# The adapter rows of half 0 wait for half 0's first values instead of its last scores

## The reference

```
x  = x + attention(conditioned(x, itok))          # 16 heads of 16, causal, softmax
g  = y @ Wg + (y @ Ag[itok]) @ Bg[itok]           # y is the new x, rank 16, 1024 hidden
u  = y @ Wu + (y @ Au[itok]) @ Bu[itok]
h  = silu(g) * u
d  = h @ Wd + (h @ Ad[itok]) @ Bd[itok]
x  = x + fwht(silu(d @ W1.T) * (d @ W3.T)) @ W2.T
```

## Time and profile before

| | |
|---|---|
| runs shown | 215.78, 216.59, 217.85 us; median 216.59 |
| profiled execution, its own time | 217.52 us |
| its span | 215.7 us |
| mean granted TensorE clock | 0.992 |
| busy: TensorE matmuls | 209.0 us (97%) |
| busy: VectorE, ScalarE, GpSimd | 96.2, 93.5, 104.5 us |
| moved by DMA | 16.65 MB, 77 GB/s mean |

### The profile page before, as it was taken

How to read it: one execution, slowest core, us unless ns; L and a number is a source line. 1 busy time by engine, 2 the same in 40 slices (tenths; PEclk the granted TensorE clock), 3 DMA queues, 4 the chain that set the end, 5 groups by cost and what they waited for, 6 DMA issues and landing times.

```text
span 215.7 us, 5107 instructions
## 1 busy us (share of the span) xinstructions
PE 209.0 (97%) x1977; PEld 167.3 (78%) x1977; DVE 96.2 (45%) x173; ACT 93.5 (43%) x162; POOL 104.5 (48%) x120
## 2 busy tenths in 40 slices
PE   7899999799999999999999999999999999999994
PEld 2567787487878788787887888788888888888894
DVE  3798998489545975210211210065942222220211
ACT  2456899446866340623532432322755554430000
POOL 4005788039693613538454349102499999441000
PEclk9999999699999999999999999999999999999999
DMA  5950099646903195031210170300111000000211
GB/s 144 393 205 3 25 145 151 81 150 143 153 0 100 50 155 143 0 104 29 74 28 18 30 310 3 97 0 0 52 41 57 2 0 3 0 0 3 97 49 49
DMA packets 16263, 16.65 MB, mean 77 GB/s; under 512 B 1776, under 2 KB 13040, under 8 KB 15984
## 3 DMA queue, kind: packets, MB, share of 16 engines
q1 hardware_dynamic: 15808, 15.26, 29.5%
q10 hardware_dynamic: 432, 1.07, 1.7%
HBM read 15.27 MB, written 1.05 MB: 76 GB/s over the span
## 4 chain that ended last, share of the span: by engine, by line
PE 92%; DMA 3%; DVE 2%; issue 1%; SPq 0%; ACT 0%
PE bank L479 25%; PE bank L481 23%; PE bank L483 23%; PE bank L636 8%; DMA raw<-w_stream 3%; PE bank L553 2%; PE bank L676 2%; PE bank L579 2%; PE bank L608 1%; PE bank L498 1%; PE bank L533 1%; PE bank L532 1%; PE bank L534 1%; PE bank L543 1%; DVE w_lo L1062 1%
## 5 line engine op out<-in xcount | busy, mean ns | idle before, releaser
L1375 POOL TENSOR_TENSOR h_lo<-tmp_b,h_hi 128x512 fp32r<-128x512 f32 x32 | 42.5, 1348 | 41.8 <-ACT h_hi L887 41.8
L479 PE MATMUL bank<-act_hi,w_hi 128*128 128x512 f32 x144 | 52.6, 402 | 0.1
L481 PE MATMUL bank<-act_lo,w_hi 128*128 128x512 f32 x144 | 51.0, 390 | 0.0
L483 PE MATMUL bank<-act_hi,w_lo 128*128 128x512 f32 x144 | 50.9, 390 | 0.0
L1199 DVE TENSOR_TENSOR tmp_b<-bank,tmp_a 128x512 f32<-128x512 f32 x32 | 20.8, 686 | 61.8 <-ACT tmp_a L894 35.8
L1328 POOL TENSOR_TENSOR w_lo<-raw,w_hi 128x512 fp32r<-128x512 f32 x21 | 26.8, 1290 | 19.7 <-ACT w_hi L822 19.7
L479 PEld LDWEIGHTS bank<-act_hi,w_hi 128*128 128x128 f32 x144 | 27.0, 188 | 7.8 <-issue 0.8
L894 ACT ACTIVATE tmp_a<-bank 128x512 f32<-128x512 f32 x32 | 17.3, 592 | 34.8 <-PE bank L636 30.6
L483 PEld LDWEIGHTS bank<-act_hi,w_lo 128*128 128x128 f32 x144 | 27.0, 188 | 5.8
L481 PEld LDWEIGHTS bank<-act_lo,w_hi 128*128 128x128 f32 x144 | 27.1, 188 | 5.1
L887 ACT ACTIVATE h_hi<-tmp_b 128x512 fp32r<-128x512 f32 x32 | 19.7, 632 | 19.9 <-DVE tmp_b L1199 19.9
(11 more groups left out here) (96 smaller groups left out, 249.8 us busy)
## 6 DMA issues: line engine op xcount, KB each, us to landing
raw<-w_stream SPq DMA_DIRECT2D x24, 256.0 KB, 3.8
b_own<-w_stream SPq DMA_DIRECT2D x32, 128.0 KB, 4.4
k_x<-x_slots ACTq DMA_DIRECT2D x2, 512.0 KB, 6.2
resid<-x_feat SPq DMA_DIRECT2D x1, 1024.0 KB, 8.1
tmp_a<-w_t SPq DMA_DIRECT2D x1, 1024.0 KB, 5.0
out_feat<-tmp_b SPq DMA_DIRECT2D x3, 256.0 KB, 2.1
a_down_raw<-w_stream SPq DMA_DIRECT2D x1, 512.0 KB, 4.3
b_down<-w_stream SPq DMA_DIRECT2D x32, 16.0 KB, 1.6
```

The costliest lines, as they stand in the source:

```text
L479: pe.matmul(ps[:, :], w[0], x_hi, start=start, stop=False)
L481: pe.matmul(ps[:, :], w[0], x_lo, start=False, stop=False)
L483: last.append(pe.matmul(ps[:, :], w[1], x_hi, start=False, stop=stop))
L1375: pool.tensor_tensor(lo, tmp_b[:, n % 4, :], f32(hi), ALU.subtract).then_inc(prod_split, 1)
```

## The change

One wait of the SP queue is another one. The 16 transfers of half 0's adapter rows were issued when the last scores of half 0 were complete; now they are issued when both tiles of half 0's first values (`values(0, 0)`) are complete. In TensorE's list this is six steps later. All else stays, and so does the order in which the SP queue issues.

```
             sp.wait_ge(xc_hi_made, DC + 1)
-            wait_full(sp, "s", 0, TILES_S - 1)
+            wait_full(sp, "y", 0, SLOTS // 2 - 1)
             load_b_own(0, 0, first_half, 0, BH)
             wait_full(sp, "s", 1, TILES_S - 1)
             for m in range(1, 4):
                 load_weights(W_GU + m)
```

## The result

The changed kernel takes 222.22 us (median of four runs, 221.24 to 222.65) against 216.67 us for the kernel before (four runs, 215.78 to 217.85). The ratio is 1.0246, with a 95% interval of 1.0186 to 1.0307: it is slower, by 5.55 us in the medians (whether by more than 2% the interval leaves open), where 3.4 us were forecast and 221.6 was the end of the range. The profiled executions took 222.40 and 217.52 us, with spans of 220.6 and 215.7: 4.9 us apart. Only these 4.9 us can be followed in the rows; the other 0.65 lie in the scatter of the four runs on either side, whose sources the rows cannot show.

A forecast was written before the change was run, and what follows sets the result against it. TensorE was taken to bound the kernel, its matmuls busy 209.0 of 215.7 us. The later gate_up(1, 0), +1.8, and the clock, +1.6, made +3.4 us on the median 216.59: 220.0 us, range 218.2 to 221.6.

The forecast's parts named there:

- What bounds the kernel, and where the gap came from: TensorE bounds; its 2.06 us gap in values(0, 1) comes from the row backlog on q1 holding up its instructions.
- When the rows go: SP starts issuing the 16 adapter rows at 33.57 us, after values(0, 0), 8.22 us later than before.
- The queue: W_GU + 1, behind the rows on SP's queue, lands at 50.55 us, 5.4 us later than before.
- the first term, +1.8: gate_up(1, 0) waits for the late W_GU + 1 and starts at 52.7 us instead of 50.88: +1.8 us.
- The gap's worth: Removing the gap in values(0, 1) gains 3.0 us, all given back in a 4.8 us stand at gate_up(1, 0).
- The clock: Clock falls behind TensorE's new gap at gate_up(1, 0): +1.6 us, bounded by 0 and about 4 us.
- The side chain: ScalarE and GpSimd start 3.6 us later, spreading ends at 65.4; adds nothing, but sets a floor of +2.7 us.
- The rule of the Trainium skill that spoke against the reading: By packet-by-packet turns between DMA queues, a full q1 would not hold q8 up for 4 us; the gap would stay.
- The range: +2.4 to 4.7 us; low end 218.2, high end 221.6 from one us more clock loss and a 0.5 later landing.
- "Slower": Whole kernel above 218.8 us, the forecast case and first rival together: chance 0.82.

The follow-up runs named there:

- half of the rows: Kernel before, with 8 of half 0's 16 adapter rows issued at the old place and 8 behind half 0's first values: 215.07 us, ratio 0.9836.
- the repetition: The changed kernel run once more, unaltered, beside the kernel before on another chip: 221.77 us, ratio 1.0199.
- twelve early rows: Kernel before, with 12 adapter rows issued at the old place and 4 behind half 0's first values: 216.72 us in one run, against 218.22.
- ten filling matmuls: Changed kernel, with 10 matmuls (results thrown away) behind gate_up(0, 0), in TensorE's gap ahead of gate_up(1, 0): 222.01 us, ratio 1.0205.
- ten early rows: Kernel before, with 10 adapter rows issued at the old place and 6 behind half 0's first values: 217.33 us in one run, against 217.5.
- the trace with 20 filling matmuls: Changed kernel, with 20 matmuls (results thrown away) behind gate_up(0, 0), in TensorE's gap ahead of gate_up(1, 0): 221.17 us, ratio 1.0126.
- the trace with the other queue: Changed kernel, with W_GU + 1 to W_GU + 3 issued from ScalarE's queue instead of SP's: 219.02 us, ratio 1.0072.

## Why the prediction was wrong

- **What bounds the kernel, and where the gap came from**: right. The gap moved with the instruction count, and went with half of the rows. The packet was late by about 2.5 us, though, and not by the 4 us that the prediction names.
- **When the rows go**: 33.57 forecast, 33.88 measured. The trace of after is 0.31 us later from its first weights on (they landed at 8.60, and at 8.30 before), long before anything changed.
- **The queue**: the first term, +1.8, was +2.44. Besides the 0.31, the 16 issues took 10.02 us instead of the 9.13 of rows 9, since one of them took 1.81 us. `W_GU + 1` was issued at 44.00 (42.7 forecast) and landed after 7.3 us at 51.3 (50.55). In the repetition `gate_up(1, 0)` started at 52.53, next to the 52.7 of the forecast. The step was right; its size varies by 0.8 us from run to run.
- **The gap's worth**: right. The whole gain of the vanished gap was given back in the stand at `gate_up(1, 0)`. That this lasted 4.79 us, with 4.8 forecast, is partly luck: both its ends came 0.6 to 0.7 us later than forecast.
- **The clock**: this is the step that failed. It was sized at 1.6 us from the only gap of the trace, and 4 us had been named as its bound. It was 2.4. The low clock lasted from 51.4 to 58.2, twice as long as before: rows 4 stop at 43 us, and with the window behind them (clock 0.92) they make 3.4 us, and 1.7 us lost rather than 1.63. The runs show that this term is no fixed price: the same program lost 1.7 us in the repetition, a gap of 2.58 us (twelve early rows) and one of 2.80 us (ten filling matmuls) lost nothing in their profiled executions, and one of 1.76 us (ten early rows) lost 1.7. It should have been a term with ends of 0 and 3.4 (6.8 us at half speed with work in all of them), not a number with 1 us about it.
- **The kernel before has the same term.** Of its runs beside the repetition, the four with a mean clock of 1.00 took 216.4 to 217.3 us, and the five with 0.99 took 217.9 to 219.2. The forecast read 3.4 us off a trace with a fall (0.992) and added them to a median of runs whose clocks are not on record. Some of the 0.65 us that the rows cannot show may lie here; that is not shown.
- **The side chain**: forecast to end at 65.4, it ended at 66.06, 0.7 us later, as the landing did. It was a floor, as said, but a higher one than +2.7, since VectorE's part of it makes TensorE wait 0.6 us more behind `values(1, 1)`. By the trace with 20 filling matmuls, the forecast landing of 50.55 gives 50.55 + 168.6 = 219.15 without any loss by the clock, nearly the span that the prediction got with 1.6 us of it. That the repetition's span (219.2) agrees with the forecast is therefore no proof of the clock's term.
- **The rule of the Trainium skill that spoke against the reading** (page "DMA: Bandwidth & Descriptors", section "Queues, rings and completion order": turns packet by packet): what the prediction drew from it, that a full q1 would not hold q8 up, does not hold here. The packet was 2.5 us late behind 16 rows and on time behind eight.
- **The range**: its top, 221.6, was 0.6 us too low. On TensorE's own path three things went wrong, 0.3 of the start, 0.3 to 0.4 of the landing and 0.8 of the clock; all went one way and make the 1.5 us by which the spans differ more than forecast. Counted by the floor, 0.75 us of it came with the late landing and 0.3 to 0.7 through the clock. The rest is the scatter of the medians. "Slower" was right.

## What to carry to other kernels

Whoever moves a burst of transfers moves the queue that stands behind it: here the rows themselves arrived in time for their user, and the next load of weights, issued only 1.7 us later than before, landed 6.2 us later. A second issuing queue did not let a load overtake rows issued before it. Look at what an in-order engine does behind the thing that comes late (ScalarE's exponentials behind its split), since that is what stays when the first wait is taken away. Where a burst is deeper than the DMA engines drain, splitting it around the two critical moments gave 1.6%, where moving it as a whole gave a loss of 2.5%. Price a fall of the clock with two ends, and add it only to a path that nothing else bounds.

## What the runs showed of the hardware

- TensorE ran dry of instructions while one DMA queue was full of 512-byte runs. The packet that brings them came at 36.2 us instead of 33 to 34, and TensorE went on 1.4 to 1.6 us after the packet's end. The gap sat at a fixed number of instructions, and 32 inserted matmuls moved it by exactly 32. Eight rows ahead of it (1 MB) did nothing; ten cost 1.76 us, twelve 2.58, sixteen 2.06 and 2.45, in one trace each.
- A load on ScalarE's queue, issued right behind a row on SP's, landed 1.0 us after that row (7.8 us after its issue); alone, such a load had taken 2.8 us.
- The adapter rows, in runs of 512 bytes, drained at about 150 GB/s with all engines busy, whereas the weight batches behind them, in runs of 1 KB, moved at 338 GB/s in the window from 50 us. The rows also go to 16 partitions each and the weights to 128, and no run tells the two differences apart.
- Whether the clock falls behind a gap varied between traces. Gaps of 1.76, 2.06, 2.45, 3.2 and 4.2 us were followed by about 3.4 us at 1.2 GHz each, one of 4.8 by 6.8 us (1.9 of them within the gap), and gaps of 2.58 and 2.80, and the 1.13 and 1.76 of the trace with the other queue, by none.
